# Attention of two later tiles: transposes moved from TensorE to VectorE and on-chip transfers, and placed one phase earlier

## The reference, cut to what matters

```python
# x, ctx: (8, 256, 256); mask: (8, 256)
def xattn(query, key, value, mask):
    scores = jnp.einsum('bqd,bkd->bqk', query, key) / sqrt(256)
    scores = where(causal or mask == 0, -inf, scores)
    return jnp.einsum('bqk,bkd->bqd', softmax(scores), value)

x = x + xattn(layernorm(x), ctx, ctx, mask)
n = layernorm(x)
h = silu(n @ w1.T * s1) * (n @ w2.T * s2)     # 256 -> 1024, ternary weights
h = gelu(h @ h1.T * sh1)                      # 1024 -> 1024
h = gelu(h @ h2.T * sh2)                      # 1024 -> 1024
x = x + h @ w3.T * s3                         # 1024 -> 256
```

## Time and profile before

| | us |
|---|---|
| median of three runs (367.99 to 369.95) | 368.64 |
| the profiled execution | 369.64 |
| its span | 367.7 |
| TensorE busy | 360.8 (98%) |
| VectorE busy | 178.4 (49%) |
| ScalarE busy | 146.7 (40%) |
| GpSimd busy | 34.1 (9%) |

### The profile page before, as it was taken

How to read it: one execution, slowest core, us unless ns; L and a number is a source line. 1 busy time by engine, 2 the same in 40 slices (tenths; PEclk the granted TensorE clock), 3 DMA queues, 4 the chain that set the end, 5 groups by cost and what they waited for, 6 DMA issues and landing times.

```text
span 367.7 us, 4722 instructions
## 1 busy us (share of the span) xinstructions
PE 360.8 (98%) x1786; PEld 304.8 (83%) x1786; DVE 178.4 (49%) x405; ACT 146.7 (40%) x247; POOL 34.1 (9%) x59
## 2 busy tenths in 40 slices
PE   8999999999999999999999999999999999999995
PEld 7787888888898888888898888888889888888884
DVE  4859235345456643433565753434545662323233
ACT  4788755842236522252133642161132653121210
POOL 7450130000100050000100004000010000000000
PEclk9999999999999999999999999999999999999999
DMA  8798999983810000000431001000001000000001
GB/s 274 259 449 350 415 371 412 365 335 118 254 44 15 3 0 29 2 0 0 134 125 59 1 0 31 0 0 2 0 0 57 3 3 0 0 0 2 0 0 62
DMA packets 12210, 38.34 MB, mean 104 GB/s; under 512 B 1762, under 2 KB 4708, under 8 KB 12004
## 3 DMA queue, kind: packets, MB, share of 16 engines
q1 hardware_dynamic: 11312, 37.11, 27.1%
q10 hardware_dynamic: 868, 0.80, 0.7%
HBM read 35.80 MB, written 13.64 MB: 134 GB/s over the span
## 4 chain that ended last, share of the span: by engine, by line
PE 97%; DVE 1%; POOL 0%; issue 0%; DVEq 0%; POOLq 0%
PE ring L983 64%; PE ring L957 16%; PE ring L1002 8%; PE att L910 2%; PE att L929 2%; PE ring L1115 1%; PE att L900 1%; PE att L918 1%; PE ring L1161 0%; PE att L1142 0%; PE ring L1142 0%; PE ring L1124 0%; POOL rstd L362 0%; DVE x_attn L722 0%; PE att L1021 0%
## 5 line engine op out<-in xcount | busy, mean ns | idle before, releaser
L983 PE MATMUL ring<-h_hi,weights 128*128 128x512 f32 x512 | 201.4, 393 | 0.2 <-issue 0.2
L983 PE MATMUL ring<-h_lo,weights 128*128 128x512 f32 x512 | 199.5, 390 | 0.0
L983 PEld LDWEIGHTS ring<-h_hi,weights 128*128 128x128 f32 x512 | 96.1, 188 | 20.5 <-DVE act L762 0.4
L983 PEld LDWEIGHTS ring<-h_lo,weights 128*128 128x128 f32 x512 | 96.1, 188 | 19.8
L519 ACT ACTIVATE act<-ring,scales 128x512 f32<-128x512 f32 x64 | 44.1, 690 | 157.9 <-PE ring L983 157.9
L775 DVE CAST h_hi<-act 128x512 fp32r<-128x512 f32 x64 | 27.7, 432 | 141.8 <-ACT act L519 132.3
L665 DVE TENSOR_TENSOR h_lo<-act,h_hi 128x512 fp32r<-128x512 f32 x96 | 66.5, 693 | 2.5
L957 PE MATMUL ring<-xn_hi,weights 128*128 128x512 f32 (+1 forms) x140 | 51.6, 375 | 0.2 <-DVE xn_lo L741 0.2
L957 PE MATMUL ring<-xn_lo,weights 128*128 128x512 f32 (+1 forms) x140 | 51.1, 371 | 0.0
L507 ACT ACTIVATE gate<-ring,scales 128x512 f32<-128x512 f32 x32 | 22.1, 691 | 33.8 <-PE ring L957 33.8
L762 DVE SCALAR_TENSOR_TENSOR act<-ring,scales,gate 128x512 f32<-128x512 f32 x32 | 24.0, 749 | 16.7 <-PE ring L957 15.4
(11 more groups left out here) (128 smaller groups left out, 217.9 us busy)
## 6 DMA issues: line engine op xcount, KB each, us to landing
weights<-weights_staged SPq DMA_DIRECT2D x11, 1024.0 KB, 9.2
x_in<-in_x SPq DMA_DIRECT2D x8, 256.0 KB, 2.8
ctx_cols<-in_ctx_cols SPq DMA_DIRECT2D x8, 256.0 KB, 4.8
ctx_rows<-in_ctx_rows SPq DMA_DIRECT2D x4, 512.0 KB, 7.5
out_dram<-residual SPq DMA_DIRECT2D x16, 128.0 KB, 1.7
turned<-in_x_cols SPq DMA_DIRECT2D x3, 512.0 KB, 8.0
mask<-in_mask SPq DMA_DIRECT2D x3, 256.0 KB
work<-means ACTq DMA_DIRECT2D x3, 256.0 KB, 3.1
```

Source lines behind the costliest of these rows:

```text
L983: ins = nc.tensor.matmul(bank[:], w, part[:, k].bitcast(dt), start=(k == 0 and part is h_hi[src]), stop=(k == HC - 1 and part is h_lo[src]))
```

## The change

For tiles 2 and 3 (prepared during tiles 1 and 2) TensorE's 14 transposes go. In their place VectorE transposes 32x32 blocks inside each 128x128 block (one instruction over all columns), and SP's queue moves the blocks to their places: 16 DMAs, one for each pair of source and target quarter of the partitions, from on-chip memory to on-chip memory, in runs of 32 elements (128 bytes). For probabilities they go from `turned` back to `work`, for normalised rows from `work` to `turned`. ScalarE and VectorE then split the rows from there, not from PSUM. Tile 1 keeps the old way.

The order of the work changes with it, in tiles 1 and 2: statistics and moments of x move into gate and up; the means are stored at its end and spread after the first chunk of layer 1; centring follows chunk 1, scores and maxima chunk 3, exponentials chunk 4 of layer 1; attention follows chunk 1 of layer 2, and normalising comes before VectorE's split of chunk 2.

The core of the diff (the parts of tile 0, which only move into a function `first_tile_step`, and the views and semaphores are left out):

```diff
@@ SyncE
                 load_values(t)
+                if t > 2:
+                    sp.wait_ge(xn_split, ROWS + PAIR * (t - 1))
                 load_query_cols(t)
+            def place_blocks(dst, src, chunks, moved):
+                to = dst[:, 0:chunks * P].rearrange("p (n i b) -> p n i b", i=BLOCKS, b=BLOCK)
+                of = src[:, 0:chunks * P].rearrange("p (n j b) -> p n j b", j=BLOCKS, b=BLOCK)
+                for i in range(BLOCKS):
+                    for j in range(BLOCKS):
+                        sp.dma_start(to[j * BLOCK:(j + 1) * BLOCK, :, i], of[i * BLOCK:(i + 1) * BLOCK, :, j]
+                                     ).then_inc(moved, 16)
+            def place_probs(t):
+                sp.wait_ge(probs_blocked, t - 1)
+                place_blocks(work, turned, PAIR * KEYS // P, probs_t_in)
+            def place_xn(t):
+                sp.wait_ge(xn_blocked, t - 1)
+                place_blocks(turned, work, ROWS * EC, xn_t_in)
...
-            for t in range(TILES - 2):
-                load_next(t + 2)
-                store(t)
-            for t in range(TILES - 2, TILES):
-                store(t)
+            load_next(2)
+            store(0)
+            place_probs(2)
+            place_xn(2)
+            load_next(3)
+            store(1)
+            place_probs(3)
+            place_xn(3)
+            store(2)
+            store(3)
@@ ScalarE
+            def split_placed_xn(t):
+                act.wait_ge(xn_t_in, 16 * MOVES * (t - 1))
+                for b in range(PAIR):
+                    toks = slice(b * SEQ, (b + 1) * SEQ)
+                    nc.scalar.activation(xn_hi[:, :, toks].rearrange("p c (r q) -> p r c q", r=2),
+                                         xn_cols[:, 2 * b:2 * b + 2], ACT.Copy).then_inc(xn_hi_ready, 1)
@@ def first_layer(t, tests=()):
+                if 0 < t < TILES - 1:
+                    store_means(t + 1)
@@ def tile(t, tests=None, more=True):
-                        if more and (layer, c) == (0, 0 if t == 0 else 2):
+                        if t == 0 and (layer, c) == (0, 0):
                             store_means(t + 1)
-                        if more and (layer, c) == (0, 2 if t == 0 else 3):
+                        if more and (layer, c) == (0, 2 if t == 0 else 0):
                             spread_means(t + 1)
-                        if more and (layer, c) == (0, HC - 1):
+                        if more and (layer, c) == (0, HC - 1 if t == 0 else 4):
                             exponentials(t + 1)
@@ VectorE
+            def turn_probs_blocks(t):
+                dve.wait_ge(probs_ready, ROWS * t)
+                nc.vector.transpose(turned[:, 0:PAIR * KEYS], work[:, 0:PAIR * KEYS]).then_inc(probs_blocked, 1)
+            def normalise_rows(t):
+                dve.wait_ge(moments, ROWS * 2 * t)
+                dve.wait_ge(rstd_ready, 2 * t)
+                for r in range(ROWS):
+                    nc.vector.tensor_scalar(xn_rows[:, r], x_attn[:, r], mean_var[:, r, 0:1], rstd[:, r:r + 1],
+                                            ALU.subtract, ALU.mult).then_inc(xn_ready, 1)
+            def turn_xn_blocks(t):
+                dve.wait_ge(xn_ready, ROWS * t)
+                nc.vector.transpose(work[:], turned[:]).then_inc(xn_blocked, 1)
@@ def first_layer(t):
+                    if 0 < t < TILES - 1 and 3 <= c < 3 + ROWS:
+                        next_stats(t + 1, c - 3)
+                    if 0 < t < TILES - 1 and c == 3 + ROWS:
+                        wait_stats(t + 1, 0, ROWS - 1)
+                        for r in range(ROWS):
+                            norm_moments(r)
@@ def tile(t, more=True):   (tiles 1 and 2)
+                            if at == (0, 5):
+                                turn_probs_blocks(t + 1)
+                            if at == (1, 2):
+                                normalise_rows(t + 1)
+                                turn_xn_blocks(t + 1)
+                            split_hidden(t, layer, c)
+                            if at == (0, 1):
+                                for b in range(PAIR):
+                                    centre(t + 1, b)
+                            if at == (0, 3):
+                                wait_scores(t + 1)
+                                for b in range(PAIR):
+                                    mask_and_max(t + 1, b)
+                            if at == (1, 1):
+                                for b in range(PAIR):
+                                    add_attention(t + 1, b)
+                                    stats_after_attention(t + 1, b)
+                                wait_stats(t + 1, 1, ROWS - 1)
+                                for r in range(ROWS):
+                                    norm_moments(r)
@@ TensorE, def attend(t, b):
-                pe.wait_ge(probs_evac[b], t)
+                if t == 1:
+                    pe.wait_ge(probs_evac[b], 1)
+                    weights_t = probs_t
+                else:
+                    pe.wait_ge(probs_t_in, 16 * MOVES * (t - 1))
+                    weights_t = later_probs_t
@@ def tile(t, dt, more=True):
-                hidden(t, 0, range(HC), dt)
+                hidden(t, 0, range(0, 4), dt)
                 if more:
                     scores(t + 1)
-                hidden(t, 1, range(0, 3), dt)
-                if more:
-                    for b in range(PAIR):
-                        turn_probs(t + 1, b)
-                hidden(t, 1, range(3, 5), dt)
+                hidden(t, 0, range(4, HC), dt)
+                hidden(t, 1, range(0, 2), dt)
                 if more:
                     for b in range(PAIR):
                         attend(t + 1, b)
-                hidden(t, 1, range(5, 8), dt)
-                if more:
-                    turn_rows(t + 1)
+                hidden(t, 1, range(2, HC), dt)
                 down(t, dt)
```

More of the change, by code:

```diff
@@ L25 @@
 P = 128
+BLOCK = 32
+BLOCKS = P // BLOCK
+MOVES = BLOCKS * BLOCKS
 BATCH, SEQ, EMB, HID = 8, 256, 256, 1024
@@ L126, in xattn_ffn @@
         probs_t = turned[:, 0:PAIR * KEYS].rearrange("p (b k) -> p b k", b=PAIR)
+        later_probs_t = probs
+        xn_rows = turned[:].rearrange("p (r d) -> p r d", r=ROWS)
+        xn_cols = turned[:].rearrange("p (r c q) -> p r c q", r=ROWS, c=EC)
         gate_scale, up_scale, h1_scale, h2_scale = (scales[:, n] for n in range(4))
@@ L207, in xattn_ffn @@
         first_xn_hi = [sem(f"first_xn_hi{r}") for r in range(ROWS)]
+        probs_blocked = sem("probs_blocked")
+        probs_t_in = sem("probs_t_in")
+        xn_blocked = sem("xn_blocked")
+        xn_t_in = sem("xn_t_in")
         up_mm = sem("up_mm")
@@ L656, in stats_after_attention, with split_placed_xn @@
                     norm_stats(r, x_attn)
+            def turn_probs_blocks(t):
[10 more added lines that the diff above has]
+                nc.vector.transpose(work[:], turned[:]).then_inc(xn_blocked, 1)
+            def split_placed_xn(t, b):
+                toks = slice(b * SEQ, (b + 1) * SEQ)
+                dve.wait_ge(xn_hi_ready, PAIR * (t - 1) + b + 1)
+                hi = xn_hi[:, :, toks].rearrange("p c (r q) -> p r c q", r=2)
+                lo = xn_lo[:, :, toks].rearrange("p c (r q) -> p r c q", r=2)
+                nc.vector.tensor_tensor(lo, xn_cols[:, 2 * b:2 * b + 2], hi.bitcast(F32), op=ALU.subtract
+                                        ).then_inc(xn_split, 1)
             def split_xn(t, b):
@@ L798, in tile @@
                         at = (layer, c) if more else None
[L799 to L815, removed]
@@ L816, in tile @@
-                        if at == (0, 5 if t == 0 else 6):
-                            for b in range(PAIR):
[L818 to L828, removed]
@@ L829, in tile @@
-                        if at == (1, HID2_CHUNKS[2][0] + 1):
-                            for r in range(ROWS):
-                                normalise(t + 1, r)
+                        if t == 0:
+                            for flag, before in ((HID1B, (0, 2)), (HID1C, (0, 4)), (HID2A, (0, 7)), (HID2B, (1, 0)),
+                                                 (HID2C, (1, 4)), (LAST, (1, 6))):
+                                if at == before:
+                                    take_flag(flag)
+                            first_tile_step(at, 0)
+                            split_hidden(t, layer, c)
+                            first_tile_step(at, 1)
+                        else:
+                            if at == (0, 5):
[3 more added lines that the diff above has]
+                                turn_xn_blocks(t + 1)
+                            split_hidden(t, layer, c)
+                            if at == (0, 1):
[12 more added lines that the diff above has]
+                                    norm_moments(r)
@@ L832, in tile, with first_tile_step @@
                 if more:
                     for b in range(PAIR):
-                        split_xn(t + 1, b)
+                        if t == 0:
```

(31 more changed lines are left out.)

8 lines of the change are left out of this document (5 added, 3 removed).

## The result

| | median us | runs | against before, 95% interval |
|---|---|---|---|
| before | 368.93 (367.99 to 370.96) | 10 | |
| after | 365.13 (364.40 to 368.44) | 10 | 0.990 (0.988 to 0.9921) |
| after, measured again on another chip | 366.22 (365.14 to 367.53) | 6 | 0.9908 (0.9875 to 0.9941) |

The change makes the kernel faster by 3.8 us in the first measurement. In the second the kernel before took 369.23 us: the medians differ by 3.0 us, and the ratio gives 3.4 us (0.9908 of 369.23 is 365.8). I had forecast 3.04.

A forecast was written before the change was run, and what follows sets the result against it. PE's gapless chain was taken to bound tiles 1 and 2. Removing transposes gave -3.04 us, all other terms 0: 368.64 - 3.04 = 365.6 us, the forecast's own range 364.9 to 366.6.

The forecast's parts named there:

- Term 1: Transposes of probabilities and normalised rows leave PE: 1.52 us for each of two tiles, -3.04 us.
- rival D: Transposes held PE longer than their chain pieces show, 6.0 us: 362.6 us; chance 0.03.
- rival E: Freed PE time isn't on the way to the end; median stays at 368.6 us; chance 0.03.
- Term 2: Scores and attention move earlier, keeping 2.62 and 2.59 us; the cover between hidden layers isn't needed: 0.
- Term 3: Statistics move into gate and up, fitting VectorE's idle time; last low part 0.6 us spare: 0, at most tenths per tile.
- Term 4: Probabilities by block transpose and sixteen SP transfers at 0.46 us land at 158.3, wanted 162.05, spare 3.7 us: 0.
- rival A: Small stalls eat the gain: issue at 0.70 to 0.80 us or late low part; 366.8 to 368.8 us; chance 0.12.
- Term 5: Normalised rows turned by 171.6, landed at 180.7, before down ends at 194.07; late from 1.17 us per issue: 0.
- my last sign of being wrong: An issue from on-chip to on-chip memory with 128 B runs costs over 0.70 us.
- SP's own queue: Tile 3's loads stand behind tile 2's placements, query columns until about 189, wanted some 24 us on: 0.
- Rival B: SP's queue throttles the placements' short runs, 1.15 us per issue, probabilities 7.3 us late per tile: 380.2 us; chance 0.11.
- C: Transfers run one after another, 1.7 us each; probabilities 14.3 us late, rows 6.8: 408 us; chance 0.03.

The follow-up runs named there:

- series 1 to 3: Changed kernel plus sixteen extra on-chip transfers each in tile 3, 32 partitions x 6 runs of 128 B, 1 of 128 B, 768 B: 0.65, 0.63, 0.66 us an issue.

## Why the prediction was right

**What bounds the kernel.** Right: PE's chain without a gap, before and after. The order alone (87.10 us a turn) and the kernel without transfers (85.51) bracket it from both sides.

**Term 1.** Right: -1.59 us a tile turn against 1.52 forecast, -3.19 in all (174.20 us for the two tiles before, 171.01 after). The surplus lies in the matmuls around them: all hidden matmuls of a tile took 29.01 + 10.90 + 7.31 + 10.93 = 58.15 us before and 14.51 + 21.77 + 21.81 = 58.09 after. The upper bound and rival D (6.0 us) are out, rival E too, since the kernel did get faster, and so is the price of 390 ns a transpose that the prediction took from the Trainium skill, page "VectorE: DVE Perf Modes", section "The three transpose paths". The medians moved by 3.8, 0.6 more than the chain; 0.988 to 0.9921 means 2.9 to 4.4 us, so 3.19 is inside, and the second measurement says 3.0 to 3.4. The profiled spans differ by 4.7 us, but 1.6 of that is not of the change: it lies behind VectorE's last instruction (367.7 - 363.98 = 3.7 us before, 363.0 - 360.85 = 2.2 after). SP waited for the last store there for 2.9 us before and 1.4 after, but 3.1 in the second profile of the very same changed kernel.

**Term 2.** Right: 14.51 + 21.77 us with the scores between chunks 3 and 4, no gap.

**Term 3.** Right, and close: the statistics fill the idle time (0.42 us ends at 119.50, the next instruction starts at 119.63), the last low part ends at 125.47 (forecast 125.7, wanted 126.38). I had named ScalarE's wait for the scaled mean; it is 1.29 us long and sets the gelu back by 0.4 us, which nobody waits for.

**Term 4.** The mechanism was right and one size wrong. Ready at 149.27 (forecast 149.2), wanted at 162.11 (162.05), block transpose 0.98 us (1.04), landing 1.9 (1.7). But an issue cost 0.65 us, not 0.46: I took the rate of seven loads from DRAM as the nearest row for transfers within the chip. The last was issued from 159.15 and landed at about 161.05, so the spare was 1.1 us, not 3.7. (A landing is counted from the start of its issue, so my sum had one issue too many: by the measured times the limit is (162.11 - 149.30 - 1.9) / 15 = 0.73 us an issue, not 0.70.) Only 0.07 of it was left, so rival A (0.70 to 0.80) was nearer than the 0.12 I gave it: that no wait came is owed to the spare, not to the price I took. The four surplus transfers showed that the limit is real.

**Term 5.** Right within its spare: blocks ready at 171.7 (171.6), the third chunk's split at 171.64 as forecast, issues 0.74 and 0.65 us in the two tiles, landed by about 185 where 192 would do. The 0.74 comes mostly of a single issue of 1.61 us; two further profiles show one of 1.38 and one of 1.11 at the same line, and no run shows why. So my last sign of being wrong, an issue over 0.70 us, did occur here, and cost nothing because this term's limit was 1.17.

**SP's own queue.** Right: loads for tile 3 from 183.57, the store behind them from 191.16, nobody waits.

**Rival B and C.** Both wrong here: the queue isn't throttled by short runs (series 1 to 3), and issues don't wait for landings. The rule on small transfers that the prediction cites from the Trainium skill, page "DMA: Bandwidth & Descriptors", section "Rules for kernel authors", names something real: the price of an issue is per transfer and not per byte (0.63 us for 4 KB as for 128 KB). But it decides nothing while the spare holds.

## What to carry to other kernels

On an engine that is 98% busy in an unbroken chain, an instruction is worth its piece of the chain, not its recorded duration (0.109 us against a recorded 0.272), and moving it to an idle engine paid that and hardly more. The price is then a deadline: write down when the replacement is ready and when it is wanted, and which single cost per transfer would break it. For blocks that change partitions, count transfers, not bytes: a way by DRAM with 5 to 8 of them was ready sooner than 16 within the chip, but beside megabytes of weights the same small store took 11 us. And a queue that an engine issues from is that engine's own time: eight issues on ScalarE's held up a gelu by 3.7 us.

## What the runs showed of the hardware that I had not expected

- An issue with both ends on the chip cost its queue 0.63 to 0.69 us in the mean of a series, whatever its shape, with a single one of 1.1 to 1.6 us now and then, whose cause stays open; a load of the same shape from DRAM 0.48; a store of such blocks to DRAM 1.79 / 4 = 0.45 in a run of four. SP's and ScalarE's queues pay it independently.
- VectorE's 32x32 block transpose of 4-byte elements took 0.98 us for 768 columns and 1.25 us for 1024, some 1.2 to 1.3 ns a column.
- After a wait of 6.2 us PE's granted clock was 0.64 over the next 4.4 us, and back at 1.00 after that; after the wait of 1.6 us in the kernel with four transfers more it was 1.00 still.
- The receipt of the last store varies between profiles of one kernel: SP waited 1.4 us for it in one and 3.1 us in another.
